# Transposing the score maxima by DMA instead of on TensorE, in a fused attention and feed-forward kernel

## What is computed

```python
x = L0_attn_x                       # (32, 256, 128)
xn = _layernorm(x, axis=-1)
# attention
q = einsum('bsd,hde->bhse', xn, wq) + bq      # k, v alike; 16 heads, e = 8
scores = softmax(einsum('bhse,bhte->bhst', q, k) * scale, axis=-1)
att = einsum('bhst,bhte->bhse', scores, v)    # then att @ wo.T + bo
# feed-forward
x_prev = xn shifted by one token
xr = mu_r * xn + (1 - mu_r) * x_prev;  xk = mu_k * xn + (1 - mu_k) * x_prev
out = sigmoid(xr @ W_r.T) * (relu(xk @ W_k.T) ** 2 @ W_v.T)
return x + attention + out
```

## Time and profile before

| | |
|---|---|
| median of 3 runs | 468.71 us (468.67 to 470.33) |
| the profiled execution | 468.32 us |
| its span in the trace | 466.2 us |
| busy: TensorE, VectorE, ScalarE, GpSimd | 449.2, 400.7, 394.1, 366.5 us |
| mean rate of the DMA engines | 130 GB/s |

### The profile page before, as it was taken

How to read it: one execution, slowest core, us unless ns; L and a number is a source line. 1 busy time by engine, 2 the same in 40 slices (tenths; PEclk the granted TensorE clock), 3 DMA queues, 4 the chain that set the end, 5 groups by cost and what they waited for, 6 DMA issues and landing times.

```text
span 466.2 us, 15769 instructions
## 1 busy us (share of the span) xinstructions
PE 449.2 (96%) x5254; PEld 275.1 (59%) x5254; DVE 400.7 (86%) x824; ACT 394.1 (85%) x896; POOL 366.5 (79%) x674
## 2 busy tenths in 40 slices
PE   6689999999999999999999999999999999999996
PEld 5245666666656666556665666566656666666554
DVE  7578999999988999899999999899998999989831
ACT  2138899999988999989998999989998999989894
POOL 6667888888888988888888888888888888887321
PEclk9558999999999999999999999999999999999999
DMA  4533465545345545344554544355545444455100
GB/s 135 158 116 99 124 162 148 142 134 150 109 140 148 157 127 155 108 132 130 148 159 129 156 139 127 104 147 155 159 137 138 136 126 125 137 151 147 51 15 24
DMA packets 86061, 60.43 MB, mean 130 GB/s; under 512 B 6224, under 2 KB 73808, under 8 KB 86032
## 3 DMA queue, kind: packets, MB, share of 16 engines
q1 hardware_dynamic: 86032, 60.06, 45.0%
HBM read 29.89 MB, written 29.36 MB: 127 GB/s over the span
## 4 chain that ended last, share of the span: by engine, by line
PE 88%; DMA 3%; issue 2%; DVE 2%; ACT 2%; SPq 1%; ACTq 0%; DVEq 0%; POOL 0%
PE bank_val L631 26%; PE bank_exp L707 18%; PE bank_max L717 11%; PE misc L736 5%; PE misc L758 4%; PE misc L646 4%; PE misc L665 3%; PE misc L747 3%; PE misc L799 3%; PE misc L792 3%; PE misc L673 2%; PE misc L773 2%; PE misc L768 1%; DMA ops<-spill 1%; DVE neg_max L557 1%
## 5 line engine op out<-in xcount | busy, mean ns | idle before, releaser
L557 DVE TENSOR_REDUCE neg_max<-bank_max 128x2 f32<-128x512 f32 x512 | 327.9, 684 | 37.9 <-PE bank_max L717 32.8
L454 ACT ACTIVATE probs<-bank_exp 128x512 f32<-128x512 f32 x504 | 273.5, 597 | 27.4 <-PE bank_exp L707 25.3
L717 PE MATMUL bank_max<-ops 48*128 48x256 bf16 x1024 | 161.5, 278 | 0.0
L707 PE MATMUL bank_exp<-ops 51*128 51x256 bf16 x1008 | 156.0, 273 | 4.2 <-issue 2.1
L631 PE MATMUL bank_val<-probs,val 128*25 128x256 f32 x2048 | 136.8, 385 | 0.8 <-ACT probs L454 0.8
L707 PEld LDWEIGHTS bank_exp<-ops 51*128 51x128 bf16 x1008 | 74.7, 95 | 66.2 <-issue 51.5
L631 PEld LDWEIGHTS bank_val<-probs,val 128*25 128x25 f32 x2048 | 50.5, 103 | 52.2 <-issue 27.0
L717 PEld LDWEIGHTS bank_max<-ops 48*128 48x128 bf16 x1024 | 77.0, 96 | 5.7
L356 POOL TENSOR_SCALAR xn<-x_in,moments,rstd 128x128 f32<-128x128 f32 x62 | 49.3, 802 | 0.0
L395 POOL TENSOR_TENSOR mixed_x<-mixed_x,xn_t 128x512 f32<-128x512 f32 x32 | 40.7, 1273 | 2.5
L370 POOL TENSOR_TENSOR qk_l<-qk_rest,qk_m 128x512 bf16<-128x512 f32 x31 | 36.0, 1163 | 2.5
(11 more groups left out here) (77 smaller groups left out, 627.9 us busy)
## 6 DMA issues: line engine op xcount, KB each, us to landing
ops<-spill SPq DMA_DIRECT2D x126, 192.0 KB, 3.4
spill<-qk_h SPq DMA_DIRECT2D x64, 192.0 KB, 3.3
spill<-qk_m SPq DMA_DIRECT2D x64, 128.0 KB, 1.9
x_in<-x SPq DMA_DIRECT2D x32, 128.0 KB, 2.2
spill<-qk_l SPq DMA_DIRECT2D x32, 128.0 KB, 1.8
y_out<-y SPq DMA_DIRECT2D x32, 128.0 KB, 1.9
ops<-shift SPq DMA_DIRECT2D x128, 6.0 KB
w<-weights SPq DMA_DIRECT2D x1, 448.0 KB, 3.0
```

Source lines behind the costliest of these rows:

```text
L454: nc.scalar.activation(probs[g % 2][:, u % G, :, :], exp_bank(u, live)[:, :, :], ACT.Exp, scale=SCALE).then_inc(exp_done[u], 1)
L557: nc.vector.tensor_reduce(out=neg_max[hf][:, :, r, pr], in_=bank_max[MAX_BANK[v]][:, :, :], axis=AX_X, op=ALU.max, negate=True).then_inc(m ...
L707: exp_mm = nc.tensor.matmul(exp_bank(u, live)[:, i, :], ops[p][rows, hf, 1, pr, i * P:(i + 1) * P], ops[p][rows, hf, 0, pr, :], start=True ...
L717: max_mm = nc.tensor.matmul(bank_max[MAX_BANK[v]][:, i, :], of[rows, max_hf, 0, max_pr, i * P:(i + 1) * P], of[rows, max_hf, 1, max_pr, :] ...
```

## The change

- `max_parts` becomes 128 x 2 x 128 (24 of each 128 columns used, the others zeroed once by VectorE), and `shift` 128 x 2 x 128. The transpositions on TensorE and the copies on ScalarE are removed, with the waits on them. SyncE issues instead one DMA transposition per half (`transpose_shift`), SBUF to SBUF, and `load_shift` waits for its landing.
- `ops` has four buffers. The rows of ones of buffers 2 and 3 are copied by four small DMAs in turn -1 (`copy_ones`).
- SyncE's order in a turn becomes: transposition of the second half of item t; stores of the high parts; shift of the second half; stores of the middle and low parts; transposition of the first half of item t+1; operands of the first half of item t+2; shift of the first half of item t+1; operands of the second half of item t+2; load of x for item t+5; store of y for item t-1.
- GpSimd splits the first half's maxima before the sum `rest` instead of after it.
- The hardware loop has five passes (turns 4 to 23) instead of six.
- SyncE and GpSimd compute one more set of wait values in each pass, ScalarE one fewer.

```diff
-LOOP = (1, 7)
+LOOP = (1, 6)
...
-        ops = [sb(f"ops{i}", [P, 2, 2, PR, S], BF16) for i in range(2)]
+        ops = [sb(f"ops{i}", [P, 2, 2, PR, S], BF16) for i in range(TURN)]
-        max_parts = [sb(f"max_parts{i}", [P, ST, 2, 3, PR], BF16) for i in range(2)]
-        shift = [sb(f"shift{i}", [2 * 3 * PR, S], BF16) for i in range(2)]
+        max_parts = [sb(f"max_parts{i}", [P, ST, P], BF16) for i in range(2)]
+        shift = [sb(f"shift{i}", [P, ST, P], BF16) for i in range(2)]
...
+            def copy_ones():
+
+                sp.wait_ge(k_filled[0], 1)
+                for i in range(2, TURN):
+                    for r in range(2):
+                        rows = slice(RG * r + KS, RG * r + KE)
+                        sp.dma_start(ops[i][rows, :, 1], ops[0][rows, :, 1]).then_inc(ones_in, 16)
...
+            def transpose_shift(half, count, before):
+                sp.wait_ge(parts_zero, 1)
+                sp.wait_ge(max_split[half], count)
+                after(sp, shift_in[half], before)
+                sp.dma_start_transpose(shift[half][:, :, :], max_parts[half][:, :, :].rearrange("p n c -> p (n c)")).then_inc(
+                    shift_done[half], 16)
+
+            def load_shift(half, c, done, before):
+
+                sp.wait_ge(shift_done[half], done)
                 after(sp, shift_in[half], before)
                 for r in range(2):
-                    sp.dma_start(ops[p][RG * r + KS:RG * r + KE, half, 0],
-                                 shift[half][3 * PR * r:3 * PR * (r + 1), :]).then_inc(shift_in[half], 16)
+                    sp.dma_start(ops[c][RG * r + KS:RG * r + KE, half, 0],
+                                 shift[half][3 * PR * r:3 * PR * (r + 1), :, :]).then_inc(shift_in[half], 16)
...
             def step(t, c, n, moved, paired, quad, live):
                 p = c % 2
-                if live(4) and live(0):
-
-                    sp.wait_ge(x_bo_done, n(0))
-                    sp.wait_ge(xn_done, n(0))
-                    load_x(t + 4, c)
-                if live(1):
-
-                    after(sp, exp_scores[H - 1], n(-1))
-                    load_ops(1, 1 - p, moved(1, SPILLS), moved(0, 2))
+                if live(0):
+                    transpose_shift(1, n(0), moved(-1, 2))
...
                 if live(0):
-                    load_shift(1, p, n(0), moved(-1, 2))
+                    load_shift(1, c, moved(0, 1), moved(-1, 2))
                 if live(2):
                     spill_part(p, "m", qk_m, (m_done, m_done), n)
                     spill_l(p, n)
-
-                    after(sp, exp_scores[HALF - 1], n(0))
+                if live(1):
+                    transpose_shift(0, n(1), moved(0, 2))
+                if live(2):
+
+                    after(sp, exp_scores[H - 1], n(-1))
                     if not live(0):
                         sp.wait_ge(k_filled[p], 1)
                     if live(1):
-                        load_ops(0, p, moved(2, SPILLS), moved(1, 2))
+                        load_ops(0, (c + 2) % TURN, moved(2, SPILLS), moved(1, 2))
...
                 if live(1):
-                    load_shift(0, 1 - p, n(1), moved(0, 2))
+                    load_shift(0, (c + 1) % TURN, moved(1, 1), moved(0, 2))
+                if live(2):
+                    load_ops(1, (c + 2) % TURN, moved(2, SPILLS), moved(1, 2))
+                if live(1) and not live(0):
+                    copy_ones()
+                if live(5) and live(1):
+                    sp.wait_ge(x_bo_done, n(1))
+                    sp.wait_ge(xn_done, n(1))
+                    load_x(t + 5, (c + 1) % TURN)
                 if live(-1):
-
-                    sp.wait_ge(y_done, n(-1))
-                    sp.dma_start(out_dram[t - 1], y[1 - p][:, :].rearrange("p (n d) -> p n d", n=ST)).then_inc(
-                        out_done[1 - p], 16)
+                    store_y(t - 1, 1 - p, n(-1))
...
-                    if u == 1 and live(0):
-                        move_shift(1, near, n(0), moved(-1, 2))
...
-                    if u == 9 and live(1):
-                        move_shift(0, far, n(1), moved(0, 2))
...
-                    if u == 1 and live(0):
-                        pe.wait_ge(max_split[1], n(0))
+                    if u == 3 and live(0):
                         pe.wait_ge(act_r_done, n(0))
                         after(pe, qk_rest_done[1], n(2))
-                        transpose_shift(1, near)
-                    if u == 3 and live(0):
-                        pe.wait_ge(shift_done[1], n(0))
...
-                    if u == 9 and live(1):
-                        pe.wait_ge(max_split[0], n(1))
+                    if u == 11 and live(1) and live(0):
                         after(pe, att_t_done, n(-1))
                         after(pe, qk_rest_done[0], n(2))
-                        if not live(0):
-                            pe.wait_ge(consts_made, 2)
-                        transpose_shift(0, far)
-                    if u == 11 and live(1) and live(0):
-                        pe.wait_ge(shift_done[0], n(1))
                         project_values(c + 1, far)
```

More of the change, by code:

```diff
@@ L170, in split_attention_ffn_kernel @@
         max_split = [sem(f"max_split{i}") for i in range(2)]
-        shift_psum = [sem(f"shift_psum{i}") for i in range(2)]
+        parts_zero = sem("parts_zero")
         shift_done = [sem(f"shift_done{i}") for i in range(2)]
@@ L234, in _, with load_ops @@
                 load_x(b, b)
-            def load_ops(half, p, spilled, before):
+            def load_ops(half, c, spilled, before):
                 after(sp, spill_done, spilled)
@@ L327, in split_max @@
                 m, zero = neg_max[half], zeros[:, :, :, :]
-                part = [max_parts[half][:, :, :, j, :] for j in range(3)]
+                parts = max_parts[half][:, :, 0:2 * 3 * PR].rearrange("p n (r j k) -> p n r j k", r=2, j=3)
+                part = [parts[:, :, :, j, :] for j in range(3)]
                 last_unit = HALF * (half + 1) - 1
                 after(pool, max_done[last_unit], count)
-                after(pool, shift_psum[half], before)
+                after(pool, shift_done[half], before)
                 nc.gpsimd.tensor_tensor(part[0], m[:, :, :, :], zero, ALU.add).then_inc(max_h[half], 1)
@@ L371, in step @@
                                             ALU.subtract).then_inc(l_done, 1)
+                if live(1):
+                    split_max(0, n(1), moved(0, 1))
                 if live(-1):
@@ L409, in step @@
                 if live(1):
-                    split_max(1, n(1), n(0))
-            steps(pool, step, (SPILLS,))
+                    split_max(1, n(1), moved(0, 1))
+            steps(pool, step, (1, SPILLS))
         @block.scalar
@@ L419, in _ @@
             act.wait_ge(weights_in, 16 * N_WEIGHT_DMAS)
-            def move_shift(half, bank, count, before):
-                act.wait_ge(shift_psum[half], count)
-                after(act, shift_in[half], before)
-                nc.scalar.copy(shift[half][:, :], shift_in_bank(bank)).then_inc(shift_done[half], 1)
             def move_values(parity, bank, count):
@@ L502, in _ @@
             nc.vector.memset(zeros[:, :, :, :], 0.0)
+            for i in range(2):
+                last = nc.vector.memset(max_parts[i][:, :, :], 0.0)
+            last.then_inc(parts_zero, 1)
             nc.vector.memset(eps[:, :], EPS)
@@ L635, in mix_values @@
                 last.then_inc(mix_psum[g], 1)
-            def transpose_shift(half, bank):
-                for st in range(ST):
-                    last = nc.tensor.transpose(shift_in_bank(bank)[:, st * P:(st + 1) * P],
-                                               max_parts[half][:, st].rearrange("p r j k -> p (r j k)"),
-                                               ident16[:, :])
-                last.then_inc(shift_psum[half], 1)
             def project_values(c, bank):
@@ L714, in step @@
                         if live(ahead):
-                            rows, of = slice(RG * (1 - r), RG * (1 - r) + KS), ops[(p + ahead) % 2]
+                            rows, of = slice(RG * (1 - r), RG * (1 - r) + KS), ops[(c + ahead) % TURN]
                             max_mm = nc.tensor.matmul(bank_max[MAX_BANK[v]][:, i, :],
```

42 lines of the change are left out of this document (19 added, 23 removed).

## The result

The median went from 469.25 us (468.67 to 470.33, 4 runs) to 482.99 us (480.58 to 486.45, 4 runs). The ratio is 1.0308, 95% interval 1.0267 to 1.035: 3% slower, where 462.6 was forecast, faster by 1.4%. The profiled execution took 486.45 us, the longest of the four, so what it shows of losses is somewhat more than the median's.

What follows compares the result with a forecast made beforehand. TensorE was taken to set the 13.27 us turn. 468.32 - 6.4 (transpositions) - 0.2 (loop boundaries) + 0.5 (start) = 462.2, plus 0.39 for the median: 462.6 us; own range 461 to 466, full range 460.5 to 485.

Steps and rivals of the forecast that it cites:

- the issue: SyncE's queue: issuing one DMA transposition was taken to hold it between 0.36 and 0.75 us.
- leg 2: SyncE's queue, first half's transposition and what follows: through at 230.4 + T, so T may be up to 3.3 us.
- rival B: Slower: a transposition holds the DMA rings, the first operand load behind it lands late; 497 us, chance 0.06.
- T: Time of a DMA transposition from the start of its issue to its landing; taken as 2.6 us.
- both legs: SyncE's queue: the second half's shift bears T up to 3.4 us, the first half's up to 3.3.
- TensorE's saving: Transpositions leaving TensorE: 0.09 to 0.10 us a pair, 64 pairs, 6.4 us in all; a turn of 13.06.
- The start: Item 1's first operand load goes out 0.15 to 0.5 us later, behind a transposition; 0.5 us lost.
- The boundaries: Loop jumps: five at 0.45 to 0.7 us against six at 0.45; taken as 0.2 us won.
- Rival A: Slower: a transposition outlasts what SyncE's queue bears, turn 2T + 6.3, deciding from T = 3.5; 489 us, chance 0.24.
- The range: 460.5 to 485 us: the forecast, the no-change case and rival A's nearer part, T up to 3.7; some 0.2 outside.

Runs made afterwards that it cites:

- order_small_dmas: order_only plus three tiny unread DMAs on SyncE's queue at each of the two places of a DMA transposition; 500.76 us, ratio 1.0708.
- order_only: The changed kernel with the transpositions left on TensorE and the copies on ScalarE; 467.06 us, ratio 0.9946 to the kernel before.
- second_half_by_dma: order_only with only the second half's maxima transposed by DMA, the first half's on TensorE; 469.47 us, ratio 1.0022.
- first_half_by_dma: order_only with only the first half's maxima transposed by DMA, ahead of the operand load; 480.41 us, ratio 1.024.
- one_block: The changed kernel with both tokens' blocks packed into one of 128 x 128, so a transposition moves half; 481.24 us, ratio 1.0252.
- load_by_act: The changed kernel with the first half's operand load issued by ScalarE behind its exponential 9 instead of by SyncE; 506.96 us, ratio 1.078.
- t0_behind_load: The changed kernel with the first half's transposition issued behind the first half's operand load instead of ahead; 555.12 us, ratio 1.187.
- loop_three_passes: The changed kernel with three hardware-loop passes instead of five, so turns 16 to 23 are written out; 491.64 us, ratio 1.0435.
- before_three_passes: The kernel before with three hardware-loop passes instead of six, so twelve more turns are written out; 471.02 us, ratio 1.0029.

## Why the prediction was wrong

**The step that failed: the issue.** I put it "between 0.36 (the store of the low part) and 0.75 (one load of the shift, half of 1.49)", by instructions of another kind. It is 1.21, above both ends. In leg 2 the operand load was to go "at 227.59 as today, or up to 227.75 if the issue takes 0.75, covered by the 0.87". The low part's store is still on time, and the parts are ready where I had them (227.70 - 0.62 = 227.08, against 227.0). But the transposition, issued 0.52 before the stores have landed, holds the load until 229.01, 0.79 after they have. 0.80 late, with 0.20 more from the longer issue of the load's first DMA and 0.24 from the landing of the second, it is 1.24 late on arrival against a room of 0.85 in that turn, and TensorE idles. The sum had the landing at its median of 3.4 and nothing for either of the two small terms. In turns 9 to 23 this takes 2.9 us, and plain turns are 13.1 to 13.6, 13.33 on average, instead of 13.06. It is the symptom that rival B named (an idle at the fifteenth pair), but not its cause: order_small_dmas shows that queue time without bytes does it. Landings past 4 us, B's other sign, occur before turn 9 (4.13 at 85.33), and in order_only too, which has no DMA transposition (4.12 at 135.04).

**The larger loss: reserve.** The test "With T = 2.6 both legs have 0.7 us or more" was made for one undisturbed turn, from one turn's rows. The queue has to live through turns in which landings and issues are longer, and the kernel before did it with some 2 us a turn of waiting for y. Of 18.5 us of span 14.3 are in turns 2 to 8 and 24 to 31, and only 0.9 in turns 9 to 23. What comes late there is the same load: its landing ends 8.6 of the 9.2 us that TensorE idles in turns 2 to 8. At 0.95 over 106 us the clock costs up to 5.3 us more, as an estimate, less what of it fell in the idles. The long idles come first in the rows, and the kernel before, without them, kept 1.00 there.

**TensorE's saving: right for a pair, smaller in the sum.** 0.09 us a pair, as second_half_by_dma's 13.17 shows. In turns 9 to 23 TensorE is busy 1.77 us less, where 3.0 (15 x 0.20) was foretold and 30 pairs at 0.09 would give 2.7; the other 0.9 I can't place.

**T: right in plain turns.** 2.3 against an assumed 2.6; outside turns 9 to 23 it goes up to 4.9. The Trainium skill (VectorE: DVE Perf Modes, The three transpose paths) gives 1309 ns for one 128 x 128 block by DMA, from which I had estimated 2.6 for two. The rows have 2.3 for two and 2.2 for one, so here the time hardly grows with the blocks. The Trainium skill's 390 ns for such a block on TensorE (same section) is not refuted by the 0.09 for a pair, as I had it: TensorE's blocks here have 24 columns, not 128. The Trainium skill's advice (same page, Rules for kernel authors), TensorE where PSUM will do, agrees with the runs: order_only has 0.9946, the change 1.0308.

**The start: mis-sized.** 0.5 foretold, 2.5 measured: 1.4 of queue (1.29 of issue, where 0.36 to 0.75 stood) and 1.1 of longer landing, which the sum did not have. TensorE's idle time there is 1.15 before, 3.82 in the changed kernel and 3.83 in order_small_dmas, which transposes nothing by DMA; in three traces that have a granted clock of 1.00 there it is 3.93 in first_half_by_dma and, with nothing ahead of that load, 1.36 in second_half_by_dma and 1.44 in order_only. So again the queue time is enough. The longer landing can't be put down to the transposition: order_only has 4.05 there without one.

**The boundaries: as foretold, as far as they can be told.** The turns 12, 16 and 20, which begin with a jump, are 13.65 to 13.96, on average 0.5 above the plain ones; 0.45 to 0.7 was foretold. The first jump falls into a disturbed turn (turn 8, 16.31).

**Rival A** did not decide: in turns 9 to 23 SyncE waited for a transposition once, 0.4 us, in the rows of its waits. Its arithmetic on the queue was the right place to look, but it asked how long the landing may take, and the loss came from the issue.

**The range.** 482.99 lies within 460.5 to 485, but in the part that stood for slow landings of the transposition (rival A, T up to 3.7), and in plain turns T is 2.3; that it lies inside is luck. The forecast's own range ended at 466.

## What to carry to other kernels

Before work is moved to a queue that issues DMAs, count the time that the queue is held, not only the landing, and treat an instruction without a row as unknown upwards as well: its cheapest neighbours are no bound. Ask what waits behind it, and keep the queue's reserve for the turns that run in new code: here late landings and long issues came with those turns, the queue without reserve passed them on to TensorE, and twice the clock fell as well. Here the best version keeps the transpositions on TensorE and takes only the new order (order_only, 0.9946).

## What the runs showed of the hardware

- A DMA transposition from SyncE holds its queue 1.21 us for two 128 x 128 blocks and 1.13 for one; the store of 128 KB next to it takes 0.36, a tiny DMA 0.62 (1.85 for three).
- It lands 2.3 us after issue (median; 2.2 for one block). The longest landings are 4.9 in the changed kernel, 5.2 in one_block and 6.1 in load_by_act; right behind two operand loads it is 3.3 (t0_behind_load, turns 9 to 23).
- Turns in code run for the first time are 1.1 us longer in the trace of loop_three_passes (14.46 against 13.39 for the same turns 16 to 23 in the changed kernel), and not in before_three_passes (13.33), whose queue has reserve.
- In the changed kernel's trace the issues of 1.4 to 2.8 us (a load of x has 0.41 else) and the low part's landings of 2.6 to 4.3 (else 1.8) all come with a transfer on an instruction queue; turns 9 to 23 have none of either.
- TensorE's granted clock fell to 1.2 GHz for part of 8 us stretches around idles of 1.8 and 3.0 us, and not around those of 0.2 to 0.4. The length alone does not decide: it stayed at 1.00 after idles of 1.3 to 1.4 us at 104, 380 and 409 us, and in order_only's trace it stayed after one of 1.6 (at 138) and fell after two of 1.0 and 0.5 (at 434 and 436).
